# Expert loop of a graph and mixture-of-experts block: two landing buffers for gathered rows, and a ScalarE copy before TensorE turns them

## The chip, the cores and the metric

The kernel runs on one core of a Trainium2 chip. The metric is the device time of one execution in microseconds (us); lower is better. The engines are named as the profile does: PE (TensorE, matrix products and transposes), PEld (its weight loads), DVE (VectorE), ACT (ScalarE), POOL (GpSimd) and SP (SyncE, which here only issues transfers).

## The reference

1250 nodes with 768 features go through a two-layer graph attention network over 20000 edges, and then through a mixture of experts. Only the second part is touched:

```python
x = x + gnn(layernorm(x), ...)
xf = layernorm(x)
ggates, gidx = topk_gates(xf @ Wg + bg, 2)               # 2 of 4 groups
elog = einsum('nd,gde->nge', xf, We) + be
egates, eidx = topk_gates(elog, 4)                       # 4 of 8 experts in each
combine = gw[:, :, None] * ew                            # a weight for each node and expert
for g in range(4):
    h = gelu(einsum('nd,edm->enm', xf, W1[g]) + b1[g])   # 768 -> 384
    o = einsum('enm,emd->end', h, W2[g]) + b2[g]         # 384 -> 768
    y = y + einsum('end,ne->nd', o, combine[:, g, :])
x = x + y
```

So each node goes through 8 of 32 experts. All is float32; the kernel splits each factor of a product in a high and a low part and sums three products.

## The kernel before

`run_experts` takes the 32 experts one after the other. `plan_experts` has put the nodes of each expert in a list (`list_i`), in tiles of 128; a tile is one column of the list. Most experts have between two and six tiles, a few have one, and there are 91 in all. Four engines run the same loop over tiles (`over_tiles`), each from its own program in its own order, tied together by semaphores; in `tile(k, e, which, start, last)` k counts the tiles, and `which` is 0 in an expert's first tile (`head`), 1 in its second, 2 in the others. Nothing schedules the work but the order in which each engine's program is written.

What happens to tile k:

- POOL gathers its 128 rows with an indirect transfer from `table` into `rows` (L1850): 768 normalised features and 32 gate weights (TW = 800 columns). POOL's `tile(u)` of tile k (L1870) does in this order: wait for DVE's split of tile k (`x_lo_made`) and for the gather of tile k+1; copy tile k+1's gates out of `rows` (`keep_gates`, L1857); copy the list's column for tile k+2 into `index` (`next_index`, L1846); wait until PE has turned tile k+1 out of `rows` (`turned`); issue the gather of tile k+2 (L1850); copy the list's column for the scatter (`to_index`, L1868); wait for the scatter before to land and for ACT's y; scatter tile k-1's result with an add into `sum_dram` (L1861).
- PE turns `rows` in six transposes into `ps_xt` (`turn_x`, L2076), as soon as the gather has landed.
- ACT copies `ps_xt` to `e_xt_hi` (L1954), DVE subtracts it from `ps_xt` to `e_xt_lo` (L2006).
- PE makes 18 products with the expert's first weights into `ps_h` (L2114), DVE adds the bias to `h_in` (L2032), ACT does gelu (L1984), PE turns the result (L2130), ACT and DVE split it (L1990, L2046).
- PE makes 18 products with the second weights into `ps_y` (`down`, L2093), ACT multiplies with the gate to `y` (`keep_y`, L1971), and POOL scatters.

PE's order in the body of tile k is: in a first tile ten small products for a list (L1424); `ps_h` of tile k, which waits for `x_lo_made`; half of `down` for tile k-1; `turn_x(k + 1)`; the other half of `down`; the turning of `h_act` for tile k.

An expert's weights are split as well, 768 columns a piece: ACT copies raw pieces to `e_hi` (L1962), DVE makes `e_lo` (L2018). The next expert's first weights are split in an expert's first tile, ACT's three pieces ahead of gelu; the second ones at the first tile's end on ACT and over the second tile on DVE. In a first tile DVE also finishes a later expert's list (`keep`, L1430 to L1441) before it splits the next tile's rows, and makes `one_row` for the list after that (L1417) right behind. SP loads weights and biases up to three experts ahead; `b1_all` is a ring of BRING bias rows.

Of the kernel before, what the change touches and what calls it, by code (L numbers as in the profile page):

```python
# [7 lines left out]
I32 = mybir.dt.int32  # L8
# [3 lines left out]
ACT = mybir.ActivationFunctionType  # L12
AX = mybir.AxisListType

P = 128
# [34 lines left out]
BRING = 8  # L50
# [1677 lines left out]
def run_experts(nc, s, w1, b1, w2):  # L1728
# [3 lines left out]
    with ExitStack() as ctx:  # L1732
# [9 lines left out]
        rows = sb("rows", [P, TW])  # L1742
        index = sb("index", [P, 1], I32)
# [19 lines left out]
        gathered, turned, x_hi_made, x_lo_made = sem("gathered"), sem("x_turned"), sem("x_hi"), sem("x_lo")  # L1763
# [42 lines left out]
        with nc.Block() as block:  # L1806
# [36 lines left out]
            def _(pool):  # L1843
                def next_index(at):

                    return nc.gpsimd.tensor_copy(index[:, :], s.list_i[:, bass.ds(at, 1)])  # L1846

                def gather():

                    nc.gpsimd.indirect_dma_start(rows[:, :], None, s.table.ap(),  # L1850
                                                 bass.IndirectOffsetOnAxis(index[:, 0:1], 0),
                                                 bounds_check=ROWS - 1).then_inc(gathered, 16)

                def keep_gates(k):

                    slot = k % RING
                    return nc.gpsimd.tensor_copy(gate[:, bass.ds(slot, 1), :].rearrange("p o c -> p (o c)"),  # L1857
                                                 rows[:, D:TW])
# [11 lines left out]
                def tile(u):  # L1870
# [5 lines left out]
                    pool.reg_mov(landed, 16 * k + 16)  # L1876
                    next_x, after_x = pool.snap(one_on), pool.snap(two_on)
                    pool.wait_ge(ready, 1)
                    pool.wait_ge(x_lo_made, next_x)
                    pool.wait_ge(gathered, 16 * k + 32)  # L1880
                    keep_gates(k + 1).then_inc(gate_kept, 1)
                    next_index(k + (LEAD + 2)).then_inc(index_set, 1)
                    pool.wait_ge(ready, 1)
                    pool.wait_ge(turned, after_x)
                    pool.wait_ge(index_set, after_x)
                    pool.wait_ge(gate_kept, after_x)
                    gather()
# [9 lines left out]
                    pool.reg_add(count, count, 1)  # L1897

                pool.sem_inc(ready, 1)
                count = pool.alloc_register("pool_tiles")  # L1900
                pool.reg_mov(count, 0)
                one_on, two_on = pool.alloc_register("one_on"), pool.alloc_register("two_on")
                free, landed = pool.alloc_register("free"), pool.alloc_register("landed")
                next_index(LEAD).then_inc(first_set, 1)
                pool.wait_ge(first_set, 1)
                gather()
# [414 lines left out]
```

## Time and profile before

| | us |
|---|---|
| median of 3 runs | 1682.17 |
| lowest and highest | 1680.57, 1683.65 |
| the profiled execution, its own time | 1680.57 |
| its span in the trace | 1678.8 |
| PE busy | 1411.9 (84%) |
| DVE busy | 1133.4 (68%) |
| ACT busy | 730.8 (44%) |
| POOL busy | 480.4 (29%) |

The expert loop fills the span from about 900 to about 1640 us. Times in the trace count from the span's start. A row of the waits names the instruction that waited, what released it, the total time, how often and the longest. A row in order of time gives the start, the length, the engine, the line and the operation, out<-in, and in brackets how long the engine was idle before it and what ended that. The length of an indirect transfer's row is the time in which POOL issues it, not that of the data. The line of a row is one of the kernel before.

### The profile page before, as it was taken

The numbers are of one execution on the slowest core, as the hardware profiler recorded it, in microseconds if no ns is written. First come the engines' busy times: TensorE is split into PE (matmuls) and PEld (weight loads), VectorE is DVE, ScalarE is ACT, GpSimd is POOL, SyncE is SP. The second block draws the span as 40 slices with busy tenths as digits, with TensorE's granted clock in tenths as the row PEclk, the third lists the DMA queues.
The fourth block names the chain that finished last, engine by engine and source line by source line (L and its number), as shares of the span: only waits on it lengthen the run. The fifth ranks groups of instructions, "written<-read, shape, count | busy, mean of one in ns | idle before, by whom it ended". The sixth has DMA issues, their size and how long they took to land. (4 is left out here: it accounts for less than half of the span.)

```text
span 1678.8 us, 30263 instructions
## 1 busy us (share of the span) xinstructions
PE 1411.9 (84%) x7585; PEld 1157.3 (69%) x7586; DVE 1133.4 (68%) x1664; ACT 730.8 (44%) x1106; POOL 480.4 (29%) x537
## 2 busy tenths in 40 slices
PE   5888888597778859799914999999999999899995
PEld 5355555352233328799913998999999899888985
DVE  5368899789999978846685455444564636675762
ACT  1355655245444533511113455444554535654650
POOL 0000000002322400011103454555554445444440
PEclk7699999779999989999956999999999999999995
DMA  4110000241121214232237888776787858998856
GB/s 154 72 60 16 16 9 16 77 188 55 64 88 59 69 47 132 66 91 101 75 105 246 218 218 214 178 166 166 178 229 178 227 131 215 244 291 211 235 105 206
DMA packets 101822, 227.39 MB, mean 135 GB/s; under 512 B 15018, under 2 KB 54186, under 8 KB 101656
## 3 DMA queue, kind: packets, MB, share of 16 engines
q1 hardware_dynamic: 78728, 146.04, 25.9%
q0 software_dynamic: 20864, 74.68, 21.3%
q10 hardware_dynamic: 2192, 6.20, 1.0%
q8 instruction: 19, 0.31, 0.1%
q14 instruction: 19, 0.16, 0.0%
HBM read 166.90 MB, written 56.05 MB: 133 GB/s over the span
## 5 line engine op out<-in xcount | busy, mean ns | idle before, releaser
L873 PE MATMUL ps_o<-prob,h_head 128*97 128x512 f32 (+1 forms) x480 | 192.5, 542 | 51.4 <-DVE prob L814 51.4
L1861 POOL DMA_INDIRECT sum_dram<-y,to_index x93 | 167.5, 1801 | 217.5 <-DMA sum_dram<-y,to_index 155.3
L2006 DVE TENSOR_TENSOR e_xt_lo<-ps_xt,e_xt_hi 128x768 fp32r<-128x768 f32 x92 | 88.1, 957 | 166.5 <-ACT e_xt_hi L1954 164.2
L2114 PE MATMUL ps_h<-e_hi,e_xt_hi 128*128 (+1 forms) x546 | 195.1, 357 | 6.2 <-DVE e_xt_lo L2006 3.3
L2093 PE MATMUL ps_y<-e_hi,e_ht_hi 128*128 (+1 forms) x546 | 192.6, 353 | 2.0 <-DVE e_ht_lo L2046 2.0
L873 PEld LDWEIGHTS ps_o<-prob,h_head 128*97 128x97 f32 x480 | 75.7, 169 | 168.3 <-issue 90.5
L2093 PE MATMUL ps_y<-e_hi,e_ht_lo 128*128 (+1 forms) x546 | 185.4, 340 | 0.0
L2114 PE MATMUL ps_h<-e_lo,e_xt_hi 128*128 (+1 forms) x546 | 185.3, 339 | 0.0
L2114 PE MATMUL ps_h<-e_hi,e_xt_lo 128*128 (+1 forms) x546 | 185.1, 339 | 0.0
L2093 PE MATMUL ps_y<-e_lo,e_ht_hi 128*128 (+1 forms) x546 | 184.9, 339 | 0.0
L2018 DVE TENSOR_TENSOR e_lo<-raw,e_hi (+1 forms) x192 | 177.6, 951 | 8.9 <-ACT e_hi L1962 8.9
L724 ACT ACTIVATE score<-score,al_col 128x1250 f32<-128x1250 f32 x80 | 106.8, 1337 | 125.5 <-DVE score L778 125.2
L1962 ACT ACTIVATE e_hi<-raw (+1 forms) x192 | 147.4, 843 | 22.5 <-PEq L1505 22.5
L504 PE MATMUL ps_c<-one_src,one_dst 128*128 x528 | 111.5, 350 | 38.2 <-issue 17.7
L1850 POOL DMA_INDIRECT rows<-table,index x93 | 102.6, 1103 | 139.8 <-PE ps_xt L2079 107.3
L1971 ACT ACTIVATE y<-ps_y,gate 128x768 f32 (+1 forms) x91 | 82.1, 902 | 115.3 <-PE ps_y L2093 65.3
L778 DVE SCALAR_TENSOR_TENSOR score<-w_room,bend 128x1250 f32<-128x1250 f32 x80 | 120.5, 1508 | 13.0 <-DMA w_room<-rel_dram 13.0
L1954 ACT ACTIVATE e_xt_hi<-ps_xt 128x768 fp32r<-128x768 f32 x92 | 74.7, 812 | 109.4 <-PE ps_xt L2079 106.1
L504 PEld LDWEIGHTS ps_c<-one_src,one_dst 128*128 x528 | 51.7, 98 | 98.3 <-issue 71.6
L2114 PEld LDWEIGHTS ps_h<-e_hi,e_xt_hi 128*128 128x128 f32 x546 | 103.9, 190 | 20.7 <-DVE e_xt_lo L2006 13.2
L814 DVE SCALAR_TENSOR_TENSOR prob<-score,count 128x1250 f32<-128x1250 f32 x80 | 115.8, 1448 | 3.4 <-PE ps_o L873 3.4
L677 POOL COPY wa_now<-wa 96x6 f32 (+1 forms) x8 | 69.1, 8649 | 164.6 <-PE ps_al L885 139.1
(337 smaller groups left out, 3029.1 us busy)
## 6 DMA issues: line engine op xcount, KB each, us to landing
raw<-in_ew SPq DMA_DIRECT2D x192, 384.0 KB
w_room<-rel_dram SPq DMA_DIRECT2D x16, 640.0 KB, 4.9
b_all<-in_eb SPq DMA_DIRECT2D x32, 192.0 KB
al_src<-al_dram SPq DMA_DIRECT2D x1, 5000.0 KB, 14.6
xs<-in_x SPq DMA_DIRECT2D x1, 3840.0 KB, 17.1
x_in_t<-in_x SPq DMA_DIRECT2D x10, 384.0 KB, 3.5
sum_dram<-x SPq DMA_DIRECT2D x10, 384.0 KB, 3.9
table<-xf SPq DMA_DIRECT2D x10, 384.0 KB, 2.3
```

Of the source, the lines that this page charges most:

```text
L504: last = nc.tensor.matmul(ps_c[:, c, 0:width], one_dst[:, m % HOTS, q, :], one_src[:, m % HOTS, q, at:at + width], start=False, stop=False)
L724: nc.scalar.activation(score[:, slot, 0:N], score[:, slot, 0:N], ACT.Exp, bias=s.al_col[:, t, bass.ds(h, 1)]).then_inc(exped, 1)
L778: nc.vector.scalar_tensor_tensor(score[:, slot, 0:N], flat[u][:, 0:N], bend[:, t, bass.ds(h, 1)], steep[u][:, 0:N], ALU.add, ALU.max).then ...
L814: nc.vector.scalar_tensor_tensor(prob[:, t % 2, 0:N], score[:, slot, 0:N], 1.0, s.count[:, t, 0:N], ALU.min, ALU.mult).then_inc(joined, 1)
L873: turn = nc.tensor.matmul(ps_o[u][0:C1 + 1, c, 0:WID[c]], h_head[:, u, t, :], prob[:, t % 2, 512 * c:512 * c + WID[c]], start=(t == 0), st ...
L1850: nc.gpsimd.indirect_dma_start(rows[:, :], None, s.table.ap(), bass.IndirectOffsetOnAxis(index[:, 0:1], 0), bounds_check=ROWS - 1).then_in ...
L1861: nc.gpsimd.indirect_dma_start(s.sum_dram.ap(), bass.IndirectOffsetOnAxis(to_index[:, w:w + 1], 0), y[:, w, :], None, bounds_check=ROWS - ...
L1962: nc.scalar.activation(hi[:, bass.ds(e % 2, 1), at:at + PIECE], raw[:, bass.ds(e % WRING, 1), at:at + PIECE], ACT.Copy).then_inc(made, 1)
L2006: nc.vector.tensor_tensor(xt_lo[:, :, :].rearrange("p (b k) n -> p b (k n)", b=2), ps_x[:, :, 0:HALF], xt_hi[:, :, :].bitcast(F32).rearran ...
L2018: nc.vector.tensor_tensor(lo[:, u, at:at + PIECE], raw[:, bass.ds(e % WRING, 1), at:at + PIECE], hi[:, u, at:at + PIECE].bitcast(F32), ALU ...
L2093: last = nc.tensor.matmul(ps_y[:, half, 0:HALF], a, b[:, bass.ds(u, 1), at:at + HALF] .rearrange("p o d -> p (o d)"), start=(c == 0 and n ...
L2114: summed = nc.tensor.matmul(ps_h[:, 0:HID], a, b[:, bass.ds(e % 2, 1), c * HID:(c + 1) * HID] .rearrange("p o m -> p (o m)"), start=(c == ...
```

## The change

The gathered rows no longer land where PE reads them. There are two landing buffers, `landed_rows[:, 0]` and `[:, 1]`, each with a semaphore of its own (`gathered[u]`), and the gates are taken out of them. ACT copies the 768 features from the landing buffer to `rows` (`copy_rows`), at the head of its tile body: it waits for the gates of that tile to be kept (`gate_kept`) and for PE's turning of the tile before (`turned`). PE's `turn_x` waits for that copy (`copied`). POOL gathers tile k+3 in the body of tile k, once tile k+1 is copied; the copy of its index now waits for DVE's split of tile k+1 (`x_lo_made`), where `keep_gates` waited for that of tile k before. The bias ring shrinks from 8 to 6 rows. The rest of the diff counts the landings of each buffer in registers, and waits for the last two gathers at the end.

```diff
-BRING = 8
+BRING = 6
...
-        rows = sb("rows", [P, TW])
-        index = sb("index", [P, 1], I32)
+        landed_rows = sb("landed_rows", [P, 2, TW])
+        rows = sb("rows", [P, D])
+        index = sb("index", [P, 2], I32)
...
-        gathered, turned, x_hi_made, x_lo_made = sem("gathered"), sem("x_turned"), sem("x_hi"), sem("x_lo")
+        gathered, copied = [sem("gathered0"), sem("gathered1")], sem("x_copied")
+        turned, x_hi_made, x_lo_made = sem("x_turned"), sem("x_hi"), sem("x_lo")
...
-                def next_index(at):
-                    return nc.gpsimd.tensor_copy(index[:, :], s.list_i[:, bass.ds(at, 1)])
-                def gather():
-                    nc.gpsimd.indirect_dma_start(rows[:, :], None, s.table.ap(),
-                                                 bass.IndirectOffsetOnAxis(index[:, 0:1], 0),
-                                                 bounds_check=ROWS - 1).then_inc(gathered, 16)
-                def keep_gates(k):
+                def next_index(at, u):
+                    return nc.gpsimd.tensor_copy(index[:, u:u + 1], s.list_i[:, bass.ds(at, 1)])
+                def gather(u):
+                    nc.gpsimd.indirect_dma_start(landed_rows[:, u, :], None, s.table.ap(),
+                                                 bass.IndirectOffsetOnAxis(index[:, u:u + 1], 0),
+                                                 bounds_check=ROWS - 1).then_inc(gathered[u], 16)
+                def keep_gates(k, u):
                     slot = k % RING
                     return nc.gpsimd.tensor_copy(gate[:, bass.ds(slot, 1), :].rearrange("p o c -> p (o c)"),
-                                                 rows[:, D:TW])
+                                                 landed_rows[:, u, D:TW])
...
+                    pool.reg_mov(arrived, 16 * pool.snap(pair) + (16 + 16 * u))
                     next_x, after_x = pool.snap(one_on), pool.snap(two_on)
                     pool.wait_ge(ready, 1)
-                    pool.wait_ge(x_lo_made, next_x)
-                    pool.wait_ge(gathered, 16 * k + 32)
-                    keep_gates(k + 1).then_inc(gate_kept, 1)
-                    next_index(k + (LEAD + 2)).then_inc(index_set, 1)
+                    pool.wait_ge(gathered[1 - u], pool.snap(arrived))
+                    keep_gates(k + 1, 1 - u).then_inc(gate_kept, 1)
                     pool.wait_ge(ready, 1)
-                    pool.wait_ge(turned, after_x)
-                    pool.wait_ge(index_set, after_x)
+                    pool.wait_ge(x_lo_made, after_x)
+                    next_index(k + (LEAD + 3), 1 - u).then_inc(index_set, 1)
+                    pool.wait_ge(ready, 1)
+                    pool.wait_ge(copied, after_x)
+                    pool.wait_ge(index_set, next_x)
                     pool.wait_ge(gate_kept, after_x)
-                    gather()
+                    gather(1 - u)
...
+                next_index(LEAD, 0).then_inc(first_set, 1)
+                next_index(LEAD + 1, 1).then_inc(first_set, 1)
+                pool.wait_ge(first_set, 2)
+                gather(0)
+                gather(1)
...
-                pool.wait_ge(gathered, 16)
-                keep_gates(0).then_inc(gate_kept, 1)
-                next_index(LEAD + 1).then_inc(index_set, 1)
-                pool.wait_ge(ready, 1)
-                pool.wait_ge(turned, 1)
-                pool.wait_ge(index_set, 1)
+                pool.wait_ge(gathered[0], 16)
+                keep_gates(0, 0).then_inc(gate_kept, 1)
+                next_index(LEAD + 2, 0).then_inc(first_set, 1)
+                pool.wait_ge(first_set, 4)
+                pool.wait_ge(copied, 1)
                 pool.wait_ge(gate_kept, 1)
-                gather()
+                gather(0)
...
+                def copy_rows(k, first=False):
+                    act.wait_ge(gate_kept, k + 1)
+                    if not first:
+                        act.wait_ge(turned, k)
+                    nc.scalar.activation(rows[:, :].unsqueeze(1),
+                                         landed_rows[:, 0:1, 0:D] if first else landed_rows[:, bass.ds(k % 2, 1), 0:D],
+                                         ACT.Copy).then_inc(copied, 1)
                 def tile(k, e, which, start, last):
                     head = which == 0
+                    copy_rows(k + 1)
...
+                copy_rows(0, first=True)
...
-                    pe.wait_ge(gathered, 16 * k + 16)
+                    pe.wait_ge(copied, k + 1)
```

The body of a tile in POOL's program (one of the two copies in the loop), before. `gate` is the copy of the gates, `index` and `to_index` the list's columns for the gather and the scatter; x_lo is `x_lo_made`, x_turned is `turned`:

```order
L1880 REGISTER_ALU [waits x_lo,h_ready]
L1857 ISA [waits gathered]
L1857 COPY gate<-rows 128x32
L1846 ISA x3
L1846 COPY index<-list_i 128x1
L1850 DMA rows<-table,index 128x800 [waits index_set,gate_kept,x_turned,h_ready]
L1888 ISA
L1868 ISA [waits scattered,h_ready]
L1868 ISA x2
L1868 COPY to_index<-list_i 128x1
L1861 DMA sum_dram<-y,to_index 1408x768 [waits y_made,scattered,to_set,h_ready]
```

and with the change (x_copied is `copied`):

```order
L1859 ISA [waits h_ready,gathered1]
L1859 COPY gate<-landed_rows 128x32
L1848 ISA [waits x_lo,h_ready]
L1848 ISA x2
L1848 COPY index<-list_i 128x1
L1852 DMA landed_rows<-table,index 128x800 [waits index_set,gate_kept,x_copied,h_ready]
L1892 ISA
L1870 ISA [waits scattered,h_ready]
L1870 ISA x2
L1870 COPY to_index<-list_i 128x1
L1863 DMA sum_dram<-y,to_index 1408x768 [waits y_made,scattered,to_set,h_ready]
```

The wait for x_lo went from ahead of the gates' copy to ahead of the index copy (and up by one tile), and the gather waits for ACT's copy instead of PE's turning; the scatter keeps its place behind the gather, and the next body's gate copy its place behind the scatter.

ACT's body of an expert's first tile, from its start to gelu, before. `e1_hi<-raw1` are the pieces of the next expert's weights:

```order
L1960 ISA [waits h_summed_2]
L1962 ISA [waits e_w1_in0]
L1962 ISA
L1962 ACTIVATE e1_hi<-raw1 128x768
L1962 ISA [waits e_w1_in1]
L1962 ACTIVATE e1_hi<-raw1 128x768
L1962 ISA [waits e_w1_in2]
L1962 ACTIVATE e1_hi<-raw1 128x768
L1981 REGISTER_ALU
L1984 ACTIVATE h_act<-h_in 128x384 [waits h_turned,biased]
```

and with the change:

```order
L1995 REGISTER_ALU [waits gate_kept]
L1996 ISA [waits x_turned]
L1996 ACTIVATE rows<-landed_rows 128x768
L1977 ISA [waits h_summed_2]
L1979 ISA [waits e_w1_in0]
L1979 ISA
L1979 ACTIVATE e1_hi<-raw1 128x768
L1979 ISA [waits e_w1_in1]
L1979 ACTIVATE e1_hi<-raw1 128x768
L1979 ISA [waits e_w1_in2]
L1979 ACTIVATE e1_hi<-raw1 128x768
L2010 ACTIVATE h_act<-h_in 128x384 [waits h_turned,biased]
```

The copy of rows, with its waits for gate_kept and x_turned, stands ahead of the three pieces and of gelu.

## Rows read from the trace of the kernel before

**Rows 1.** Waits of PE, 900 to 1660 us: who waited for whom, total us, times, longest

```profile
PE ps_xt L2079 <- DMA rows<-table,index: 33.1, 21, 11.2
```

**Rows 2.** The tile ps_xt: count, shortest/median/longest ns, first and last start us

```profile
L2079 PE MATMUL ps_xt<-ident,rows x552: 270/272/476, 901.6 to 1632.8; 128*128 128x128 f32 x184
L1954 ACT ACTIVATE e_xt_hi<-ps_xt x92: 792/812/814, 903.2 to 1633.1; 128x768 fp32r<-128x768 f32 x92
L2006 DVE TENSOR_TENSOR e_xt_lo<-ps_xt,e_xt_hi x92: 956/958/959, 904.0 to 1634.0; 128x768 fp32r<-128x768 f32 x92
```

**Rows 3.** The tile ps_lists: the columns of rows 2

```profile
L1424 PE MATMUL ps_lists<-token_now,one_row x310: 171/171/222, 902.9 to 1604.2; 128*128 128x20 bf16 x155
```

**Rows 4.** PE in order of time, 1207 to 1238 us: start, length, operation

```profile
1213.39 0.81 PE L2079 MATMUL ps_xt<-ident,rows 128*128 128x128 f32 x6
...
1215.62 0.49 PE L2130 MATMUL ps_ht<-ident,h_act 128*128 128x128 f32 x3
...
1220.90 0.81 PE L2079 MATMUL ps_xt<-ident,rows 128*128 128x128 f32 x6
```

**Rows 5.** POOL in order of time, the same stretch; in brackets idle time and releaser

```profile
1213.22 0.98 POOL L1846 COPY index<-list_i 128x1 int32 x1 [0.18 <-issue]
1215.17 1.08 POOL L1850 DMA_INDIRECT rows<-table,index  x1 [0.97 <-PE ps_xt L2079]
1216.26 1.35 POOL L1868 COPY to_index<-list_i 128x1 int32 x1
1218.50 1.60 POOL L1861 DMA_INDIRECT sum_dram<-y,to_index  x1 [0.89 <-POOL to_index L1868]
...
1223.69 0.76 POOL L1868 COPY to_index<-list_i 128x1 int32 x1
1225.68 2.31 POOL L1861 DMA_INDIRECT sum_dram<-y,to_index  x1 [1.22 <-ACT y L1971]
...
1234.98 1.96 POOL L1861 DMA_INDIRECT sum_dram<-y,to_index  x1 [3.60 <-DMA sum_dram<-y,to_index]
```

**Rows 6.** POOL in order of time, 940 to 950 us

```profile
942.84 1.60 POOL L1861 DMA_INDIRECT sum_dram<-y,to_index  x1 [2.99 <-DMA sum_dram<-y,to_index]
944.40 0.26 POOL L1857 COPY gate<-rows 128x32 f32 x1
```

**Rows 7.** Line L1846, the copies of an index: the columns of rows 2

```profile
L1846 POOL COPY index<-list_i x93: 177/514/1767, 892.4 to 1630.7; 128x1 int32 x91, 128x1 int32<-128x1 int32 x2
```

**Rows 8.** Lines L1850's gathers: what ended POOL's idle time before them

```profile
  POOL index L1846: 23.5, 24
```

**Rows 9.** Line L1861, the scatters: what ended POOL's idle time before them

```profile
  DMA sum_dram<-y,to_index: 155.3, 53
```

**Rows 10.** ACT in order of time, 1207 to 1238 us

```profile
1209.78 2.31 ACT L1962 ACTIVATE e_hi<-raw  x3
1213.33 0.53 ACT L1984 ACTIVATE h_act<-h_in 128x384 f32<-128x384 f32 x1 [1.24 <-DVE h_in L2032]
```

**Rows 11.** DVE in order of time, 1207 to 1238 us

```profile
1214.65 0.17 DVE L1441 SCALAR_TENSOR_TENSOR list_i<-found 128x10 f32 x1
1215.09 0.96 DVE L2006 TENSOR_TENSOR e_xt_lo<-ps_xt,e_xt_hi 128x768 fp32r<-128x768 f32 x1 [0.27 <-ACT e_xt_hi L1954]
...
1216.09 1.48 DVE L1417 TENSOR_TENSOR one_row<-lanes,row_in_tile 128x1280 bf16<-128x1280 bf16 x1
...
1222.59 0.96 DVE L2006 TENSOR_TENSOR e_xt_lo<-ps_xt,e_xt_hi 128x768 fp32r<-128x768 f32 x1 [1.64 <-ACT e_xt_hi L1954]
1223.47 0.95 DVE L2018 TENSOR_TENSOR e_lo<-raw,e_hi  x1
...
1225.57 0.95 DVE L2018 TENSOR_TENSOR e_lo<-raw,e_hi  x1
```

**Rows 12.** PE in stretches: busy us, granted clock, DMA share, GB/s

```profile
1339.00:1341.00 2.00, 0.54 (x5) 1.00 1.07 364
1341.00:1343.00 2.00, 2.00 (x11) 0.60 1.03 172
```

More of the change, by code:

```diff
@@ L1897, in tile @@
                     pool.reg_add(count, count, 1)
+                    if u:
+                        pool.reg_add(pair, pair, 1)
                 pool.sem_inc(ready, 1)
-                count = pool.alloc_register("pool_tiles")
+                count, pair = pool.alloc_register("pool_tiles"), pool.alloc_register("pool_pairs")
                 pool.reg_mov(count, 0)
+                pool.reg_mov(pair, 0)
                 one_on, two_on = pool.alloc_register("one_on"), pool.alloc_register("two_on")
                 free, landed = pool.alloc_register("free"), pool.alloc_register("landed")
-                next_index(LEAD).then_inc(first_set, 1)
-                pool.wait_ge(first_set, 1)
-                gather()
+                arrived = pool.alloc_register("arrived")
+                next_index(LEAD, 0).then_inc(first_set, 1)
[3 more added lines that the diff above has]
+                gather(1)
                 nc.gpsimd.memset(y[:, :, :], 0.0).then_inc(first_set, 1)
                 nc.gpsimd.tensor_copy(to_index[:, 1:2], s.list_i[:, 0:1]).then_inc(to_set, 1)
-                pool.wait_ge(first_set, 2)
+                pool.wait_ge(first_set, 3)
                 pool.wait_ge(to_set, 1)
@@ L1912, in _ @@
                 pool.sem_inc(y_made, 1)
-                pool.wait_ge(gathered, 16)
-                keep_gates(0).then_inc(gate_kept, 1)
-                next_index(LEAD + 1).then_inc(index_set, 1)
-                pool.wait_ge(ready, 1)
-                pool.wait_ge(turned, 1)
-                pool.wait_ge(index_set, 1)
+                pool.wait_ge(gathered[0], 16)
[3 more added lines that the diff above has]
+                pool.wait_ge(copied, 1)
                 pool.wait_ge(gate_kept, 1)
-                gather()
+                gather(0)
                 begin = pool.value_load(s.starts[0:1, E - 1:E], min_val=LEAD, max_val=LIST - NT)
@@ L1933, in _ @@
                     tile(0)
+                    pool.reg_mov(arrived, 16 * pool.snap(pair) + 32)
+                    pool.wait_ge(ready, 1)
+                    pool.wait_ge(gathered[1], pool.snap(arrived))
                 n = pool.snap(count)
@@ L1946, in _ @@
                 last = pool.snap(free)
-                pool.wait_ge(gathered, last)
                 pool.wait_ge(scattered, last)
+                pool.reg_mov(landed, 16 * pool.snap(pair) + 16)
+                pool.wait_ge(ready, 1)
+                pool.wait_ge(gathered[1], pool.snap(landed))
+                pool.reg_mov(landed, 16 * pool.snap(pair) + 32)
+                pool.wait_ge(ready, 1)
+                pool.wait_ge(gathered[0], pool.snap(landed))
             @block.scalar
```

## Prediction

> **What bounds the kernel now.** I read the waits of PE first, then the tile ps_xt, then each engine in order of time over four tiles of the expert loop. ps_xt is written once per tile: 552 transposes, six a tile, are 92 turnings of gathered rows, the first at 901.6 us and the last at about 1632.7 [rows 2]. So the 91 steps from tile to tile take 731 us, 8.03 us each. PE sets that pace: between two undisturbed turnings lie 7.51 us [rows 4], in which PE waits for nothing. The only wait of size is that for gathered rows, 33.1 us in 21 pieces [rows 1], and 11.2 us of it is the very first gather, which the change leaves alone. So 22 us, 1.3%, is all that a deeper gather can give back.
>
> What must be seen beside it is how tightly POOL and DVE stand around that pace. In a tile without weights the turning starts at 1220.90 and DVE's e_xt_lo, the last piece that the next tile's matmuls need, ends at 1222.59 + 0.96 = 1223.55: 2.65 us later [rows 4, 11]. PE then does 18 matmuls and half of the previous tile's output before it turns again: 7.51 - 2.65 = 4.86 us. Everything that the change puts between e_xt_lo and the next turning is free up to 4.86 us, and costs in full beyond it.
>
> **The change, part by part.** 1. The gather moves from "after the turning of tile k+1" to "after e_xt_lo of tile k+1", since POOL's wait for x_lo goes up by one and now stands ahead of the index copy. It fetches tile k+3 instead of k+2, so its landing has more than a tile of room. The 22 us of PE's waits go.
>
> 2. ScalarE gets a copy of 128x768 per tile. Nothing in the trace is the same; near it are e_xt_hi out of PSUM, 0.81 us [rows 2], and e_hi<-raw between buffers, 2.31 us for three, 0.77 each [rows 10]. I take 0.81; 0.77 to 0.90 are the ends.
>
> 3. The wait that matters is a new one. The copy of tile k+1's rows waits for POOL's copy of its gates (gate_kept), and POOL does that only after tile k-1's body, in strict order: index, gather, next scatter index, scatter, and then the gates. The turning waits for ScalarE's copy. Before, the turning waited for the gather's landing alone, and POOL's late scatters and gate copies held up nobody but the next gather. Now there is a closed ring with one tile's distance: e_xt_lo -> index copy -> gather -> scatter index -> scatter -> gate copy -> ScalarE's copy -> turning -> e_xt_hi -> e_xt_lo. Its steps, each at its shortest:
> - from e_xt_lo's end to the index copy: 0.04 for the signal and 0.18, the gap ahead of that copy when POOL waits for nothing [rows 5]; the copy 0.18 [rows 7]
> - to the gather's start 0.97 (in the row of 1215.17; the 24 gathers that waited for the index copy waited 23.5 us, 0.98 each [rows 5, 8]); the gather 1.08 [rows 5]
> - the scatter index, the same kind of copy, 0.18; from its end to the scatter 0.89 [rows 5]
> - from the scatter's start to the end of the gate copy 944.66 - 942.84 = 1.82 [rows 6]
> - 0.04 and ScalarE's copy 0.81, 0.04 to the turning, and 2.65 to e_xt_lo's end
>
> That is 0.40 + 0.97 + 1.08 + 0.18 + 0.89 + 1.82 + 0.85 + 0.04 + 2.65 = 8.88 us. The part before the turning is 6.23 us against the 4.86 us that PE covers: PE waits 1.37 us in every tile. The output y isn't late in it: a scatter that waited for y started 1225.68 - 1220.90 = 4.8 us after the turning [rows 4, 5], and the ring brings POOL there at 6.2. 91 steps of 8.88 are 808 us.
>
> 4. In the first tile of an expert the ring is longer. There are 31 with a list to make (310 matmuls into ps_lists, ten each [rows 3]). ScalarE's order is now: copy of rows, three pieces of weights, gelu, e_xt_hi; DVE follows with the pieces' low parts, h_in, the list, and only then e_xt_lo. From ScalarE's first piece at 1209.78 to the end of list_i at 1214.82 are 5.04 us [rows 10, 11]. Before, that run began as soon as ScalarE had finished the previous tile and lay under PE's work. Now it begins behind the copy, which comes just before the turning: e_xt_lo ends 5.04 + 0.03 + 0.96 = 6.03 us after the copy, not 0.04 + 2.65 = 2.69: +3.34. And right behind e_xt_lo of such a tile DVE makes one_row: 1216.09 to 1217.57, and POOL's small copy of 1216.26 took 1.35 us and ended with it, at 1217.61 [rows 5, 11]. The index copy now falls on the same place, and ends 1.56 us after e_xt_lo instead of 0.40: +1.16. Together 4.50 x 31 = 140 us.
>
> 5. In the second tile DVE makes a low part of weights right behind e_xt_lo (1223.47 to 1224.42), and POOL's copy ended with it again (1223.69 + 0.76); the scatter beside the next such part took 2.31 us and not 1.60 [rows 5, 11]. The index copy loses 0.5 us there, and the gather meets the second part for 0 to 0.7. I take 0.9 in 30 tiles: 27 us; the ends are 0 and 1.2 x 30 = 36.
>
> The page "SBUF — State Buffer" of the Trainium skill (section "A bandwidth-pool intuition that's wrong (but worth ruling out)") says that while VectorE holds the shared port, GpSimd can't write descriptors at all until VectorE's end and about 0.115 us. The scatter's row shows 0.71 more beside a part of 0.95. By the page's rule the gather would wait 0.95 + 0.12 and the second tile would cost 0.5 + 1.07, 47 us in 30 tiles instead of 27: 20 us more in the sum.
>
> 6. Scatters still go one after another. 53 of them waited for the one before to land, 155.3 us in all [rows 9]; one that started at 1225.68 let the next go at 1234.98, 9.3 us later [rows 5]. In the ring such a wait lies on the path, but a step is now 8.9 us and longer, so only landings over that cost: 0 to 20 us, I take 0. The bias ring of six instead of eight buffers has no wait that comes near it, and costs nothing. The start gets one copy and one gate copy ahead of the first turning, 1 us.
>
> **Sum.** 808 + 140 + 27 = 975 us for the steps that take 731 now: +244, and +1 at the start. The profiled execution took 1680.57 us around its span of 1678.8, 1.6 below the median of the runs. 1680.6 + 245 = 1925.6; I say **1925 us**.
>
> **Rivals.** (a) It does what double buffers usually do: the gates and the copy are ready early, the ring doesn't close, and PE loses only its waits: 1680.6 - 22 = 1659, faster. For it speaks that POOL is idle before most scatters [rows 9]; against it the order of waits, since POOL can't reach the next gate copy before the scatter. It decides at the ring's 4.86 us: the 5.34 us from e_xt_lo to the end of POOL's gate copy alone are over it. The page "Trainium Kernel Development and Optimization" of the Trainium skill (section "Best Practices") advises double buffers for performance, to overlap transfers with work, which is this case's expectation.
> (b) The ring is there but shorter: POOL's gaps of 0.97 and 0.89 are hidden because its queue runs ahead. Then 6.23 - 1.86 = 4.37 us fits under 4.86, and only the first tiles cost, by 3.34 + 1.16 less the 0.49 of room: 4.0 x 31 = 124, less 22: 1783. Against it: the gaps stand in the rows after copies that the next instruction waits for, which stay.
> (c) The first tiles don't add: then 808 + 27 is +104 + 1, 1786. It would need the weights' pieces to stand ahead of the copy; the order shows them behind.
> (d) The clock falls as well. Around one late gather PE was busy 0.54 of 2 us, and in the next 2 us the granted clock was 0.60 [rows 12], so half speed (1.2 GHz) for most of them. If PE's short waits did this in every tile, its 4.86 us would grow by about 1.7 to 6.6, 0.4 over the ring, and the turning by 0.8: 1.2 x 91 = 109, at 2035.
>
> **How the numbers follow.** The forecast 0.83, (a) 0.04, (b) 0.04, (c) 0.03, (d) 0.05, and 0.01 for no change: gains and costs cancel. The forecast's own ends: below, without items 5 and the index delay of item 4 (27 + 36) it is 1862; above, with 36 instead of 27, 20 for landings, ScalarE's copy at 0.90 (8) and a fallen clock behind the first tiles alone (31 x 0.8 = 25) it is 1987. The range is 1860 to 1985. A measurement of this kernel tells 0.2% from no change: faster 0.04, same 0.01, slower 0.95.
>
> **What would show it.** Steps of about 8.9 us in tiles without weights, and 13.4 for the step behind an expert's first turning; PE's wait for gathered rows replaced by a wait for ScalarE's copy, some 1.4 us a tile; ScalarE's copy waiting for POOL's gate copy; the index copy waiting for e_xt_lo, and beside one_row lasting over 1 us. Wrong would be: steps of 7.5 us in plain tiles (the ring doesn't close), POOL idle ahead of its gate copies, or a granted clock well under 1 through the loop.

## The result

The changed kernel takes 1962.65 us (median of 4 runs, 1959.59 to 1964.04) against 1681.37 us before: 1.168 times as long, with an interval of 1.164 to 1.171. That is 281 us more, where 245 were forecast; it lies within the range, 38 us over the forecast of 1925.

The profiled execution's span is 1962.2 us. From its page, the busy time of PE, DVE, ACT and POOL, with the share of the span, and the granted clock of PE in 40 slices of the span:

```profile
span 1962.2 us, 30468 instructions
...
PE 1487.8 (76%) x7585; PEld 1208.9 (62%) x7586; DVE 1131.9 (58%) x1664; ACT 795.0 (41%) x1198; POOL 458.9 (23%) x539
...
PEclk7899996999997999956989999999998998888886
```

ScalarE has 64 us more to do. PE is busy 76 us longer with the same 7585 instructions, mostly since its granted clock was lower (0.93 on average from 950 to 1850 us, against 0.99 from 950 to 1600 before); what that cost is worked out further down. Neither adds up to 281 us, and DVE and POOL have no more to do than before. So I looked at the waits. The waits of PE from 900 us on (total us, times, longest) are:

```profile
PE ps_xt L2106 <- ACT rows L1996: 156.9, 87, 13.7
PE ps_h L2141 <- DVE e_xt_lo L2033: 42.2, 28, 1.6
PE ps_ht L2157 <- ACT h_act L2010: 36.4, 28, 1.5
```

The 33.1 us for gathered rows of [rows 1] are gone, and 156.9 us of waits for ScalarE's copy stand in their place, in 87 of the 92 turnings. The other two rows, 79 us together, are waits in the first tiles of the experts; before, PE had 3.3 us of the one and none of the other. The tile ps_xt gives the length of the loop, and who waited for whom around it:

```profile
L2106 PE MATMUL ps_xt<-ident,rows x552: 272/273/476, 902.2 to 1913.5; 128*128 128x128 f32 x184
...
  POOL index L1848: 502.5, 91
```

902.2 to about 1912.8 us are 1010.6 us for the 91 steps that took 731 before [rows 2], about 280 more: the whole difference lies there. And POOL, none of whose idle time was put down to DVE before, idled 502.5 us before its index copies until e_xt_lo was made, in all 91 tiles. The tile landed_rows says that ScalarE's copy waited 412.2 us for POOL's gate copies, and its last line gives the time from a gather's issue to its landing: 7.7 us at most, where the gate copy that needs it starts some 12 us behind a gather, so no landing was late.

```profile
  ACT rows L1996: 412.2, 91
...
DMA to landing us min/median/max: 3.8/4.1/7.7
```

One turn of the ring can be read off in order of time. POOL, over a tile without weights and, after the dots, behind an expert's first tile:

```profile
1267.45 0.18 POOL L1848 COPY index<-list_i 128x1 int32 x1 [4.35 <-DVE e_xt_lo L2033]
1268.62 1.08 POOL L1852 DMA_INDIRECT landed_rows<-table,index  x1 [0.98 <-POOL index L1848]
1269.70 0.20 POOL L1870 COPY to_index<-list_i 128x1 int32 x1
1270.79 1.60 POOL L1863 DMA_INDIRECT sum_dram<-y,to_index  x1 [0.89 <-issue]
1271.85 0.76 POOL L1859 COPY gate<-landed_rows 128x32 f32 x1
...
1289.72 1.07 POOL L1848 COPY index<-list_i 128x1 int32 x1 [7.58 <-DVE e_xt_lo L2033]
```

ACT, with the copy of the plain tile and that of a first tile, which has the three pieces of weights behind it:

```profile
1272.86 0.84 ACT L1996 ACTIVATE rows<-landed_rows 128x768 f32 x1 [4.30 <-POOL gate L1859]
...
1282.37 0.84 ACT L1996 ACTIVATE rows<-landed_rows 128x768 f32 x1 [4.34 <-POOL gate L1859]
1283.12 2.30 ACT L1979 ACTIVATE e_hi<-raw  x3
```

DVE, with e_xt_lo of two plain tiles and the end of a first tile:

```profile
1266.00 0.96 DVE L2033 TENSOR_TENSOR e_xt_lo<-ps_xt,e_xt_hi 128x768 fp32r<-128x768 f32 x1 [3.73 <-ACT e_xt_hi L1971]
...
1275.51 0.96 DVE L2033 TENSOR_TENSOR e_xt_lo<-ps_xt,e_xt_hi 128x768 fp32r<-128x768 f32 x1 [4.51 <-ACT e_xt_hi L1971]
...
1287.97 0.17 DVE L1441 SCALAR_TENSOR_TENSOR list_i<-found 128x10 f32 x1
1288.27 0.96 DVE L2033 TENSOR_TENSOR e_xt_lo<-ps_xt,e_xt_hi 128x768 fp32r<-128x768 f32 x1
...
1289.26 1.49 DVE L1417 TENSOR_TENSOR one_row<-lanes,row_in_tile 128x1280 bf16<-128x1280 bf16 x1
```

PE, with a turning mostly at half speed, two at full speed, and the turning of h that waits for gelu in a first tile:

```profile
1254.17 1.42 PE L2106 MATMUL ps_xt<-ident,rows 128*128 128x128 f32 x6 [2.02 <-ACT rows L1996]
...
1273.75 0.87 PE L2106 MATMUL ps_xt<-ident,rows 128*128 128x128 f32 x6 [1.79 <-ACT rows L1996]
...
1283.27 0.87 PE L2106 MATMUL ps_xt<-ident,rows 128*128 128x128 f32 x6 [1.64 <-ACT rows L1996]
...
1287.23 0.55 PE L2157 MATMUL ps_ht<-ident,h_act 128*128 128x128 f32 x3 [1.52 <-ACT h_act L2010]
```

e_xt_lo ends at 1266.96; index copy 1267.45, gather 1268.62, scatter index 1269.70, scatter 1270.79, gate copy done at 1271.85 + 0.76 = 1272.61; ScalarE's copy 1272.86, turning 1273.75, e_xt_lo 1275.51, ended 1276.47. One turn took 9.51 us, and it has no wait in it but those for the link before.

Two of the links, 0.49 us from e_xt_lo to the index copy and 0.25 from the gate copy to ScalarE's, are longer than the 0.04 or 0.05 of the others that are mere signals. The instructions before the copies show why. "POOLq" and "ACTq" are the engine's sequencer, which runs the wait and the register instructions ahead of an operation; the columns are those of [rows 2], for the one tile above:

```profile
L1885 POOLq EVENT_SEMAPHORE  x1: 17/17/17, 1267.0 to 1267.0; - x1
...
L1848 POOLq FUSED_REGOPS  x2: 37/117/197, 1267.1 to 1267.3; - x2
L1848 POOLq SEQ_ASSERT  x1: 18/18/18, 1267.3 to 1267.3; - x1
...
L1995 ACTq ALU_OP  x1: 38/38/38, 1272.6 to 1272.6; - x1
...
L1996 ACTq FUSED_REGOPS  x1: 90/90/90, 1272.7 to 1272.7; - x1
```

POOL's wait for e_xt_lo (L1885) was over at once, at 1267.0, 0.03 us after e_xt_lo's end. Then came three register instructions for the index copy (197, 18 and 37 ns, with gaps), and the copy started at 1267.45. ACT's first instruction behind POOL's gate copy started 0.03 us after its end as well, and its own copy 0.21 later, behind one more register instruction. By the code, these register instructions work out which column of the list and which landing buffer is meant.

The lengths of all 91 steps, taken from one end of e_xt_lo to the next in order of time and sorted by the kind of tile, give a table for both kernels. "Into a first tile" is the step that ends with e_xt_lo made in an expert's first tile, "out of it" the one after. Of the 33 of the first row, 19 have no piece of weights in them at all; their median is 7.50 before and 9.52 after.

| step | count | before, median (sum) us | after, median (sum) us |
|---|---|---|---|
| neither | 33 | 7.50 (252) | 9.53 (321) |
| into a first tile | 27 | 7.79 (213) | 12.78 (345) |
| out of a first tile | 27 | 8.36 (223) | 10.44 (287) |
| both (an expert of one tile) | 4 | 10.57 (42) | 14.45 (58) |

### The profile page after: what moved, and what is told of

Its sections match the earlier page's. It is cut to its first block and busy times, and to the rows that moved or that the text cites. A ratio compares the mean times of both kernels' runs of the same rounds, so it can differ in the third digit from the quotient of the medians.

```text
span 1962.2 us, 30468 instructions
## 1 busy us (share of the span) xinstructions
PE 1487.8 (76%) x7585; PEld 1208.9 (62%) x7586; DVE 1131.9 (58%) x1664; ACT 795.0 (41%) x1198; POOL 458.9 (23%) x539
## 5 line engine op out<-in xcount | busy, mean ns | idle before, releaser
L1996 ACT ACTIVATE rows<-landed_rows 128x768 f32 (+1 forms) x92 | 77.5, 842 | 412.2 <-POOL gate L1859 412.2
L2141 PE MATMUL ps_h<-e_hi,e_xt_hi 128*128 (+1 forms) x546 | 209.4, 383 | 42.5 <-DVE e_xt_lo L2033 42.2
L2106 PE MATMUL ps_xt<-ident,rows 128*128 128x128 f32 x552 | 86.1, 295 | 157.0 <-ACT rows L1996 156.9
L2141 PE MATMUL ps_h<-e_lo,e_xt_hi 128*128 (+1 forms) x546 | 198.8, 364 | 0.0
L2141 PE MATMUL ps_h<-e_hi,e_xt_lo 128*128 (+1 forms) x546 | 198.2, 363 | 0.0
L1848 POOL COPY index<-list_i 128x1 int32 (+1 forms) x94 | 52.1, 555 | 540.3 <-DVE e_xt_lo L2033 502.5
L2106 PEld LDWEIGHTS ps_xt<-ident,rows 128*128 128x128 f32 x552 | 62.1, 146 | 185.2 <-ACT rows L1996 185.1
L1863 POOL DMA_INDIRECT sum_dram<-y,to_index x93 | 151.0, 1624 | 89.8 <-issue 83.9
L2141 PEld LDWEIGHTS ps_h<-e_hi,e_xt_hi 128*128 128x128 f32 x546 | 114.5, 210 | 55.1 <-DVE e_xt_lo L2033 54.4
L1852 POOL DMA_INDIRECT landed_rows<-table,index x94 | 102.9, 1094 | 92.7 <-POOL index L1848 75.0
```

What stands on the lines that cost most here:

```text
L1852: nc.gpsimd.indirect_dma_start(landed_rows[:, u, :], None, s.table.ap(), bass.IndirectOffsetOnAxis(index[:, u:u + 1], 0), bounds_check=ROW ...
L1863: nc.gpsimd.indirect_dma_start(s.sum_dram.ap(), bass.IndirectOffsetOnAxis(to_index[:, w:w + 1], 0), y[:, w, :], None, bounds_check=ROWS - ...
L2106: last = nc.tensor.transpose(ps_x[:, c // 3, (c % 3) * P:(c % 3 + 1) * P], rows[:, c * P:(c + 1) * P], s.ident[:, :])
L2141: summed = nc.tensor.matmul(ps_h[:, 0:HID], a, b[:, bass.ds(e % 2, 1), c * HID:(c + 1) * HID] .rearrange("p o m -> p (o m)"), start=(c == ...
```

## The experiments

The theory was that of the prediction: the ring over POOL's body and ScalarE's copy. The rivals were that ScalarE's copy itself, the place of its work, colliding transfers, or the clock cost the time.

### Opening the ring

```diff
-                    pool.wait_ge(gathered[1 - u], pool.snap(arrived))
-                    keep_gates(k + 1, 1 - u).then_inc(gate_kept, 1)
+                    pool.wait_ge(gathered[u], pool.snap(arrived))
+                    keep_gates(k + 2, u).then_inc(gate_kept, 1)
```

(the landing that it waits for is counted one further, and tile 1's gates are kept ahead of the loop, behind tile 0's)

> Edit, against the changed kernel: POOL copies the gates of tile k+2 at the head of the body of tile k, one tile earlier than it did, so ScalarE's copy of tile k+1's rows no longer waits for the scatter of the body just before. Buffers, gathers three tiles ahead and ScalarE's copy all stay. Theory A (the ring from e_xt_lo over POOL's body, the gate copy and ScalarE's copy back to the turning sets the pace, 9.53 us a plain tile): the ring now spans two tiles, PE's 7.5 us a tile is the bound again, PE waits for ScalarE's copy for under 10 us in all, and the time is 1650 to 1690 us. Rival B (ScalarE's extra 0.84 us a tile, or the order of ScalarE's work, is what costs): it stays above 1850. Rival C (gathers three tiles ahead collide with scatters and weight loads): it stays above 1850 too, with landings as late as in the changed kernel.

Measured: 1684.23 us, 1.0015 times the kernel before (1.000 to 1.003). The waits of PE:

```profile
PE ps_h L2143 <- DVE e_xt_lo L2035: 21.1, 24, 1.6
...
PE ps_xt L2108 <- ACT rows L1998: 13.7, 1, 13.7
```

The one wait left for the copy is the first tile's at the start. Plain steps are 7.50 us. POOL itself waits for much now (140.3 us for the scatter before to land and 28.0 for gathered rows, from 930 to 1640 us), and it holds up nobody. All the buffers, the gathers three tiles ahead and ScalarE's copy are still there, so rivals B and C fall: 278 of the 281 us hung on the place of one small copy in POOL's program. But nothing is gained over the kernel before either. Steps into a first tile take 8.6 us on average against 7.9 before; that is the wait for e_xt_lo, 21.1 us, and comes from ScalarE's copy, which stands ahead of the weights there.

### The place of ScalarE's copy in first tiles

```diff
-                    copy_rows(k + 1)
                     if head and not last:
                         if not start:
                             act.wait_ge(h_summed, k)
                         weights(e + 1, 0)
+                    copy_rows(k + 1)
```

> Edit, against the changed kernel: in an expert's first tile ScalarE copies the rows behind the three pieces of weights instead of ahead of them. The ring stays closed. Theory A: the pieces run while ScalarE would wait for the gate copy, so the step of a first tile loses its surcharge of 3.25 us (12.78 against 9.53), 31 times: 1962 - 100 = 1860 us, with plain steps still at 9.5. Rival D (the surcharge comes from DVE's list and one_row, not from the place of ScalarE's copy): above 1940.

Measured, in the changed kernel with the ring closed: 1892.51 us, 1.125 times the kernel before (1.123 to 1.128), 70 us under the changed kernel. Steps into a first tile went from 12.78 to 10.39 us, and plain ones stayed at 9.55. PE's waits:

```profile
PE ps_xt L2106 <- ACT rows L1996: 201.1, 91, 13.7
...
PE ps_h L2141 <- DVE e_xt_lo L2033: 4.0, 3, 1.6
```

The waits for e_xt_lo and gelu are gone from first tiles (42.2 and 36.4 us before the edit). So the place of the copy was what cost there, and rival D falls. But 2.4 us of the 3.25 came back, not all, and the time is 32 us over the 1860 expected. POOL in order of time in such a tile shows where 0.66 of the other 0.84 us went:

```profile
1264.96 0.86 POOL L1870 COPY to_index<-list_i 128x1 int32 x1
```

DVE in order of time, at the same place:

```profile
1264.81 1.83 DVE L2045 TENSOR_TENSOR e_lo<-raw,e_hi  x2 [0.52 <-ACT e_hi L1979]
```

The copy of the scatter's index took 0.86 us instead of 0.20, while DVE made the low parts that now run early. It is one of the ring's links. In this run it took 0.6 to 1.0 us in nearly every first tile.

Both edits together:

> Both edits: gates one tile early, and the copy behind the weights in first tiles. Theory A: as the first edit alone with the first tiles' DVE chain 0.8 us earlier: 0.4 us in each of 31 first tiles, so 5 to 15 us under the first edit alone, 1640 to 1680. If the copy then comes too late for the turning in first tiles, no gain over it or up to 10 us of loss.

Measured: 1669.90 us, 0.993 times the kernel before (0.991 to 0.996). That is 293 us under the changed kernel. Over the kernel before it is a small gain, 13 us, but the interval leaves 1 out. In order of time PE turns at its own pace, and its waits for e_xt_lo fell from 21.1 to 4.2 us:

```profile
1208.38 0.82 PE L2108 MATMUL ps_xt<-ident,rows 128*128 128x128 f32 x6
...
1215.88 0.82 PE L2108 MATMUL ps_xt<-ident,rows 128*128 128x128 f32 x6
```

Its waits, in total from 900 us on:

```profile
PE ps_xt L2108 <- ACT rows L1998: 20.6, 7, 13.7
...
PE ps_h L2143 <- DVE e_xt_lo L2035: 4.2, 6, 1.6
```

The same kernel was run again beside a further edit:

> The kernel with the gates one tile early and the copy behind the weights, again, on the same chip as the one with the early scatter index: 1665 to 1675 us, and 10 to 16 us under the kernel before.

1667.86 us, 0.992 (0.989 to 0.994).

### The copy with a single landing buffer

```diff
+                def copy_rows(k, first=False):
+                    act.wait_ge(gathered, 16 * k + 16)
+                    if not first:
+                        act.wait_ge(turned, k)
+                    nc.scalar.activation(rows[:, :], landed_rows[:, 0:D], ACT.Copy).then_inc(copied, 1)
...
-                    pool.wait_ge(turned, after_x)
+                    pool.wait_ge(copied, after_x)
```

(in the kernel before; the copy at the head of ScalarE's body, and PE's turning waits for it)

> Edit, against the kernel before: one landing buffer, ScalarE copies it to the fixed buffer at the head of its tile body and waits for the landing itself, not for the gate copy; the gather of tile k+2 goes out once tile k+1 is copied, which is some 5 us earlier than once it is turned. POOL's order stays that of before. Theory A (ScalarE's copy by itself costs nearly nothing, only the way over POOL does): 1660 to 1700 us. Rival B (the copy itself costs 0.84 us or more on the path, in each tile): 1681 + 77 = 1758 or more.

Measured: 1735.09 us, 1.032 (1.029 to 1.035). Neither number was right. Plain steps are 7.51, so the copy itself costs nothing there, as theory A has it; but steps into a first tile take 9.2. The waits of all engines from 950 to 1650 us:

```profile
ACT rows L1980 <- DMA landed_rows<-table,index: 110.4, 65, 3.8
...
DVE e_lo L2027 <- ACT e_hi L1963: 54.4, 25, 4.1
```

ScalarE stood 110 us before its copy until the rows had landed, and in first tiles its pieces of weights, and DVE's behind them, stood with it. With the copy behind the weights:

> Edit, against the kernel with one landing buffer and ScalarE waiting for the landing: in first tiles ScalarE copies behind the three pieces of weights. There its wait for the landing held up the pieces, and first tiles took 9.5 us against 7.7. Theory A (ScalarE's order is what that kernel paid for): it loses 31 x 1.5 = 46 us and comes to 1675 to 1700, near the kernel before. If a single landing buffer is itself too little, it stays above 1715.

Measured: 1694.42 us, 1.008 (1.005 to 1.010), within the expectation: 41 us back. PE's wait for the copy is 41.6 us in 27 pieces there (12.1 of it at the start), against 20.6 in 7 with two landing buffers. So the second buffer with gathers three tiles ahead, and the gates taken early, are worth 25 us together, once the ring is open; no run parts the two.

### Links of the ring made shorter

```diff
-                                         landed_rows[:, 0:1, 0:D] if first else landed_rows[:, bass.ds(k % 2, 1), 0:D],
+                                         landed_rows[:, 0:1, 0:w] if first else landed_rows[:, bass.ds(k % 2, 1), 0:w],
```

(with w = D for the first tile and 128 for the others; the other 640 columns of `rows` are left as they were)

> Edit, against the changed kernel: ScalarE copies only the first 128 of the 768 columns of each tile (all 768 for the first). The other columns of later tiles are left out, so what is computed from them is old rows; instructions and waits stay. Near rows: ScalarE's operations on 384 columns take 0.48 to 0.53 us and those on 768 take 0.77 to 0.84, so 128 columns should take about 0.25 to 0.3. Theory A (the copy is a serial link of the ring): plain steps go from 9.5 to about 8.95, 91 x 0.55 = 50 us less, 1912 us (1900 to 1925). Rival E (the step is set by something beside the copy, as scatters landing one after another or the clock): under 15 us of change.

Measured: 1919.62 us, 43 under the changed kernel. The copy, and its length (shortest, median, longest in ns):

```profile
L1997 ACT ACTIVATE rows<-landed_rows x92: 295/309/842, 902.2 to 1869.3; 128x128 f32 x91, 128x768 f32<-128x768 f32 x1
```

It is 842 - 309 = 533 ns shorter, and the plain step went from 9.53 to 9.00: the step gave back all that the link gave up. That is what a ring does, and rival E falls.

```diff
                     keep_gates(k + 1, 1 - u).then_inc(gate_kept, 1)
+                    own, rest = pool.snap(free), pool.snap(landed)
+                    pool.wait_ge(ready, 1)
+                    pool.wait_ge(scattered, own)
+                    next_to_index(k, u).then_inc(to_set, 1)
```

(and the same four lines taken out behind the gather)

> Edit, against the changed kernel: POOL copies the scatter's index at the head of its tile body, right behind the gates, where it waits anyway, and not between gather and scatter. Theory A in its strong form (the copy of 0.20 and the whole gap of 0.89 behind it lie on the ring): the step loses up to 1.1 us, 100 us in all, 1862. In its weak form (the gap belongs to the start of any indirect transfer, whatever stands before it): it loses the copy's 0.20 alone, 18 us, 1944, and POOL still idles 0.9 ahead of the scatter. Rival E (POOL's body isn't on the path): no change.

Measured: 1901.07 us, 62 under the changed kernel, between the two forms. POOL, gather and scatter:

```profile
1267.93 1.08 POOL L1852 DMA_INDIRECT landed_rows<-table,index  x1 [0.99 <-POOL index L1848]
1269.32 1.60 POOL L1863 DMA_INDIRECT sum_dram<-y,to_index  x1 [0.31 <-issue]
```

The gather ends at 1269.01 and the scatter starts 0.31 later, where 0.20 of copy and 0.89 of gap stood. So two thirds of that gap belong to the wait for the copy, and 0.3 to the start of the scatter. The steps without a piece of weights lost all of the 0.78 us that the link gave up: their median went from 9.52 to 8.72. (Over all 33 of the table's first row it is 8.96, since in the others DVE's pieces still hold up the index copy.) The steps out of first tiles gave back only 0.26 (10.18), for a reason that wasn't traced; most of what 62 us lack of 91 x 0.78 lies there.

The same edit with the ring open:

> Edit, against the kernel with the gates one tile early and the copy behind the weights (1669.9 us): POOL also copies the scatter's index at the head of its body. In the changed kernel this took 61 us off, since that copy and a part of the gap behind it lay on the ring. Theory A: with the ring opened POOL's body is off the path, so nearly nothing of that is left: within 5 us of 1670. If POOL's body still sets the pace in some tiles it gains up to 20 us; if scatters that go out earlier delay a gather's landing it loses as much.

Measured: 1674.76 us, 0.996 (0.994 to 0.998), where the kernel without it had 1667.86 on the same chip. Nothing of the 62 us is left, as it should be once the ring isn't the bound. It is even 7 us slower than without the edit; PE waited 26.9 us for the copy, against 21.5, and the rest of the 7 us wasn't traced.

### DVE beside POOL's index copy

```diff
-                    if head and not last:
-                        match_rows(nc, s, e + AHEAD).then_inc(rows_made, 1)
-                    elif which == 1:
+                    if which == 1:
...
                                             ALU.subtract).then_inc(h_lo_made, 1)
+                    if head and not last:
+                        match_rows(nc, s, e + AHEAD).then_inc(rows_made, 1)
```

> Edit, against the changed kernel: in first tiles DVE makes token_now and one_row behind e_ht_lo and not right behind e_xt_lo. Theory F (POOL's index copy lasts 1.07 us there and not 0.18 because DVE's one_row runs at that time): the index copy takes 0.18 to 0.2 us behind first tiles too, the step behind loses 0.9, 31 x 0.9 = 28 us, 1935. Rival G (the copy is slow there for POOL's own reasons): no change of the copy's length and of the time. The list is needed only an expert later, so nothing waits for it longer, unless an expert has one tile.

Measured: 1991.43 us, 29 slower and not 28 faster. POOL in order of time, the index copy and the next scatter index:

```profile
1303.14 1.53 POOL L1848 COPY index<-list_i 128x1 int32 x1 [7.58 <-DVE e_xt_lo L2033]
...
1306.75 0.85 POOL L1870 COPY to_index<-list_i 128x1 int32 x1
```

DVE in the same stretch:

```profile
1303.15 1.48 DVE L1417 TENSOR_TENSOR one_row<-lanes,row_in_tile 128x1280 bf16<-128x1280 bf16 x1
...
1306.61 0.95 DVE L2045 TENSOR_TENSOR e_lo<-raw,e_hi  x1
```

e_ht_lo had nothing to wait for and took 0.55 us at once, so that one_row ran from 1303.15 to 1304.63, right over the index copy that POOL had begun 0.01 before. The copy took 1.53 and ended at 1304.67, 0.04 after one_row, as the one in the changed kernel ended at 1290.79 with one_row's 1290.75. And the whole body had slid so far that the scatter index fell on DVE's next piece of weights: 0.85 us, ending at 1307.60 with the piece's 1307.56. The edit was badly made, since it didn't move one_row out of the way. But it moved one_row's end by about 0.5 us against the copy's start, and the copy's end went with it: behind each of the 31 first tiles the index copy took 1.5 us where it had taken 1.07. In the changed kernel the copy ended 0.04 us after DVE's instruction in all 31 of these tiles. So theory F holds as to the cause, and the time that it would give back wasn't measured.

## Why the prediction was right

**The ring** was the mechanism, and the steps show it. Item 3 gave 8.88 us for a plain step; it was 9.53 (median). Link by link from the rows above, forecast and measured: e_xt_lo's end to the index copy 0.22 and 0.49; copy 0.18 and 0.18; to the gather 0.97 and 0.99; gather 1.08 and 1.08; scatter index 0.18 and 0.20; to the scatter 0.89 and 0.89; scatter to the end of the gate copy 1.82 and 1.82; to ScalarE's copy 0.04 and 0.25; the copy 0.81 and 0.84; to the turning 0.04 and 0.05; turning to e_xt_lo's end 2.65 and 2.72. All that was read from rows of the same operation held within 0.02 but for the last. What failed is the price of two links: from e_xt_lo's end to the index copy it was 0.27 us too low, and from the gate copy's end to ScalarE's copy 0.21. With 0.03 for the copy and 0.07 for the last link that is 0.58 of the 0.65 us by which the step was short. That is 59 us over 91 steps, more than the whole miss of 38.

It wasn't the signal that was mis-sized. The waiting sequencer went on 0.03 us after the end of what it waited for in both places, as the prediction's 0.04 has it. What the prediction left out are the register instructions between the wait and the copy. It took 0.18 for them from a row of before, in which the wait for x_lo stands ahead of the gate copy. There the same three instructions started at 1212.8, beside that gate copy (1212.82 to 1213.03), and only their end showed as a gap:

```profile
L1846 POOLq FUSED_REGOPS  x2: 53/122/192, 1212.8 to 1213.1; - x2
```

In the changed kernel the wait stands right ahead of them, so that they lie on the ring in full. The order of POOL's instructions ahead of the prediction shows it (the "L1848 ISA" lines behind the wait for x_lo). No run moved them ahead of the wait, so what that would give back isn't measured.

**First tiles** (item 4) were 4.50 us dearer by the forecast. The part of ScalarE's order is 12.78 - 9.53 = 3.25 for a forecast of 3.34; that of one_row 10.44 - 9.53 = 0.91 for 1.16, since the index copy starts 0.27 later anyway. 31 times 4.16 is 129 us for 140.

**Second tiles** (item 5) were put at 0.9 us in 30 tiles and are 0.2 to 0.3 in 27. In the changed kernel, the index copy lasts 0.41 there instead of 0.18 (POOL's copy of 1300.15, as DVE's piece of weights ran from 1299.57 to 1300.52):

```profile
1300.15 0.41 POOL L1848 COPY index<-list_i 128x1 int32 x1 [4.38 <-DVE e_xt_lo L2033]
```

The gather's part didn't come. The gather of this tile took 1.08 us, as alone, though DVE's second piece ran beside it:

```profile
1301.55 1.08 POOL L1852 DMA_INDIRECT landed_rows<-table,index  x1 [0.99 <-POOL index L1848]
...
1301.74 0.95 DVE L2045 TENSOR_TENSOR e_lo<-raw,e_hi  x1
```

The 94 gathers together took 102.9 us, 1.09 each. The sentence that the prediction took from the page "SBUF — State Buffer" of the Trainium skill (section "A bandwidth-pool intuition that's wrong (but worth ruling out)") is about a `tensor_copy` on VectorE; DVE's pieces here are subtractions. Carried over to them, as the prediction did, it would have cost 47 us, and this trace doesn't bear that out. Item 5 comes to 7 us for a forecast of 27.

**Landings** (item 6) cost nothing, as taken: the one wait of POOL for a scatter's landing, 4.1 us, comes behind the loop. **The clock**, rival (d) and the upper end of the range, had a small part. The turning at 1254.17 above took 1.42 us and its e_xt_lo ended 3.26 after it, not 2.72. The stretches around it (busy, granted clock, DMA share, GB/s), half speed (1.2 GHz) for most of two of them:

```profile
1254.00:1256.00 2.00, 1.83 (x8) 0.59 0.77 129
1256.00:1258.00 2.00, 2.00 (x8) 0.56 0.81 155
1258.00:1260.00 2.00, 2.00 (x15) 1.00 0.00 0
```

By the median plain step, the three terms make 91 x 9.53 + 129 + 7 = 1003 of the 1010.6 us; 8 us are left for this and all else. Half speed costs time only where PE lies on the ring, from the turning to e_xt_lo. In 12 of the 60 steps that don't end in a first tile this way took 2.83 to 3.38 us and not 2.72, with turnings of 0.99 to 1.54 us and not 0.87: 4.3 us in all. Elsewhere PE's slower products lay under POOL's part of the ring: behind the first tile's turning of 1283.27 all 18 products into ps_h ran at half speed (0.52 us each for 0.34), and the next turning still began 0.05 us after ScalarE's copy. So of the 76 us that PE was busy longer about 4 cost time; this is read from one trace, and no run has the slower clock taken away alone. Of the other 4 us, 3.2 us are three scatters that started 0.9 to 1.4 us late for no reason that the rows show.

**The sum**: + 59 for the ring, - 11 for first tiles, - 20 for second ones and + 8 for the rest is + 36, for the 1010.6 against 975 us of the loop. Of the rivals, (a) needed the gates ahead of the scatter: with them there the time was 1684 and not 1659, since the gain of 22 us went to the copy ahead of the weights in first tiles, and to 1668 once that was mended. (b) was closest to something real: the gap of 0.89 is hidden in part when the copy ahead of it is moved, but not by itself. (c) had the order wrong; and with the order that it asked for (the copy behind the weights, ring closed) the time was 1892.51 and not 1786. The plain step of 9.54 us for 8.88 is 60 us of that, and first tiles still added 0.6 us on the way in and 0.9 behind one_row.

## What to carry to other kernels

Before a buffer is added, follow the release of the copy into it backwards through the program order of every engine on the way: a semaphore that is raised at the head of an engine's next body is raised only after all that stands in the body before. If that way comes back to the operation itself within one tile, its links add up to a ring, and the step can't be shorter than their sum. The cheapest mend here was to raise the same semaphore one tile earlier; that a third buffer wouldn't have helped follows from the order and wasn't tried. Count among the links what stands between a wait and its operation, register instructions too. And the same small operation costs most at the head of an in-order engine's body: with the ring open, steps into first tiles took 8.6 us with the copy ahead of the weights and 7.8 behind them, against 7.9 in the kernel before, which has no copy.

## What was new about the hardware

- From DVE's end to a POOL copy it took 0.49 us, and from POOL's end to an ACT copy 0.25. The signal was 0.03 us of each; the rest were register instructions between the wait and the copy. The three ahead of POOL's copy, 197, 18 and 37 ns with their gaps, make nearly all of its 0.49.
- An indirect transfer started 0.89 to 0.99 us after a POOL copy that it waited for, and 0.31 after the transfer before it when there was no such copy between them.
- A POOL copy of 128 x 1 elements, 0.18 us by itself, lasted 0.41, 0.85, 1.07 and 1.53 us beside DVE instructions with two inputs in SBUF, and ended 0.04 us after them, in the changed kernel in all 31 tiles beside one_row and all 27 beside a piece of weights. An indirect gather beside the same kind of instruction took its usual 1.08 us.
- PE's granted clock fell to half speed for stretches of the loop, in which PE waited 1.7 us a tile for the copy on average and 4.0 at most; its mean was 0.93, against 0.99 before. PE was busy 76 us longer by it, and about 4 us of that reached the time.
